# Two semaphores in place of one for the later rows of the fine index: what the change does to an adjacency kernel on one core

## The reference, cut to what matters

```python
def _L0_gnn_ref(x, adj, mask, W1, b1, W2, b2):
    ...
    nd = adj_d > 0
    vals = jnp.where(nd[..., None], x[:, None, :, :], jnp.inf)
    s = jnp.sort(vals, axis=2)
    nv = nd.sum(2)
    agg = jnp.zeros_like(x)
    for tau, w in zip(TAUS, WTS):
        pos = jnp.asarray(tau, x.dtype) * jnp.maximum(nv - 1, 0).astype(x.dtype)
        lo = jnp.floor(pos).astype(jnp.int32)
        hi = jnp.ceil(pos).astype(jnp.int32)
        ...
        agg = agg + jnp.asarray(w, x.dtype) * (v_lo + frac * (v_hi - v_lo))
    ...
    h = jax.nn.relu(out @ W1 + b1)
    y = h @ W2 + b2
...
x = _layernorm(x + _L0_gnn_ref(x, adj, nodemask, ...), axis=-1)
```

## Time and profile before

| | us |
|---|---|
| median of 3 runs | 3416.59 |
| lowest and highest of them | 3411.93, 3427.28 |
| the profiled execution, its own time | 3415.25 |
| span of that execution in the trace | 3413.5 |
| busy: PE, DVE, ACT | 2304.1, 2806.8, 1993.9 |

### The profile page before, as it was taken

How to read it: one execution, slowest core, us unless ns; L and a number is a source line. 1 busy time by engine, 2 the same in 40 slices (tenths; PEclk the granted TensorE clock), 3 DMA queues, 4 the chain that set the end, 5 groups by cost and what they waited for, 6 DMA issues and landing times.

```text
span 3413.5 us, 45704 instructions
## 1 busy us (share of the span) xinstructions
PE 2304.1 (67%) x16234; PEld 1004.3 (29%) x16234; DVE 2806.8 (82%) x5398; ACT 1993.9 (58%) x3077; POOL 12.4 (0%) x24
## 2 busy tenths in 40 slices
PE   0000015667878787878878787878778787866996
PEld 0000002223333333323333333323233333213764
DVE  7999998978788888879788887878797888635776
ACT  2112432466867676867768676867677676741232
POOL 0000000000000000000000000000000000000000
PEclk6555557788888888989889888888888888876777
DMA  3001000000000101010000101010000000000011
GB/s 63 0 0 48 6 0 19 7 23 19 20 19 20 31 11 28 13 32 11 28 19 19 20 20 30 11 33 9 31 12 27 19 20 19 5 23 25 26 37 37
DMA packets 126915, 72.05 MB, mean 21 GB/s; under 512 B 95512, under 2 KB 110058, under 8 KB 126698
## 3 DMA queue, kind: packets, MB, share of 16 engines
q1 hardware_dynamic: 122570, 68.23, 7.8%
q10 hardware_dynamic: 4128, 1.05, 0.2%
HBM read 41.05 MB, written 15.58 MB: 17 GB/s over the span
## 4 chain that ended last, share of the span: by engine, by line
PE 38%; SPq 20%; DVE 20%; ACT 12%; issue 7%; DMA 2%; DVEq 0%; ACTq 0%
SPq L403 20%; PE ring L623 8%; PE rows L662 7%; ACT hot L1075 6%; PE found_bank L674 5%; PE bcast L636 4%; DVE keys L1324 2%; DVE keys L1323 2%; ACT prod L1068 2%; PE bank L916 2%; DVE delta L1364 1%; DVE delta L1362 1%; DVE perm L1366 1%; DVE perm L1367 1%; PE bcast L754 1%
## 5 line engine op out<-in xcount | busy, mean ns | idle before, releaser
L1075 ACT ACTIVATE hot<-bcast,consts 128x1024 f16<-128x1024 f32 x744 | 831.5, 1118 | 129.3 <-PE bcast L636 129.1
L623 PE MATMUL ring<-member,neigh_t 128*128 128x512 bf16 x2048 | 543.8, 410 | 22.5 <-DVE member L1412 13.0
L1068 ACT ACTIVATE prod<-rows 128x512 f32<-128x512 f32 x720 | 431.6, 599 | 195.0 <-PE rows L662 195.0
L662 PE MATMUL rows<-hot,table 128*64 128x512 f16 x3072 | 526.2, 424 | 0.0
L651 PE MATMUL rows<-fine_rows,consts 32*128 32x512 bf16 x768 | 318.6, 415 | 207.7 <-DMA fine_rows<-turned 207.4
L636 PE MATMUL bcast<-idx_t,consts 32*128 32x512 f16 x1488 | 310.8, 414 | 158.5 <-ACT hot L1075 157.1
L623 PEld LDWEIGHTS ring<-member,neigh_t 128*128 128x128 bf16 x2048 | 193.3, 104 | 342.0 <-issue 135.5
L561 PE MATMUL ring<-identb,adj_b 128*128 128x128 bf16 x256 | 35.1, 274 | 368.9 <-ACT adj_b L971 357.6
L674 PE MATMUL found_bank<-prod,consts 128*32 128x512 f32 x1536 | 239.8, 701 | 11.2 <-ACT prod L1068 10.5
L1493 DVE TENSOR_SCALAR picked<-cnt,above 128x960 bf16<-128x960 f16 x192 | 78.7, 467 | 193.8 <-PE bcast L745 180.4
L1521 DVE TENSOR_TENSOR picked<-picked 128x3072 uint16<-128x3072 uint16 (+2 forms) x192 | 209.5, 1091 | 11.2
(11 more groups left out here) (347 smaller groups left out, 4424.1 us busy)
## 6 DMA issues: line engine op xcount, KB each, us to landing
late<-in_adj_dram SPq DMA_DIRECT2D x16, 1024.0 KB, 5.4
adjt_d<-neigh_t SPq DMA_DIRECT2D x16, 512.0 KB, 2.7
fine_rows<-turned SPq DMA_DIRECT2D x512, 8.0 KB
fine_rows<-turned SPq DMA_DIRECT2D x512, 16.0 KB
turned<-adjt_d SPq DMA_DIRECT2D x16, 512.0 KB, 3.7
adj_s<-adjt_d SPq DMA_DIRECT2D x16, 512.0 KB, 3.6
xt_d<-keys SPq DMA_DIRECT2D x2, 1024.0 KB, 10.5
parts_d<-parts SPq DMA_DIRECT2D x4, 512.0 KB, 6.9
```

The costliest lines, as they stand in the source:

```text
L623: ins = mm(ring[u % 2][:, :], kept_t[:, j, P * i:P * i + P], member[:, j, n // 2, 512 * (n % 2):512 * (n % 2) + 512], start=(j == 0), stop ...
L662: ins = mm(rows[u % 2][C * h:C * h + C, :], table[:, s, GROUPS * h + g8, :], hot[:, u % HOT, h, :], start=False, stop=(s == 1), skip_group ...
L1068: run(prod[:, u % DEEP, :], rows[u % 2][:, :], ACT.Relu).then_inc(S["prod_by_act"], 1)
L1075: run(hot[:, u % HOT].rearrange(flat), spread_bank(l, u)[0][:, 0:2, :].rearrange(flat), ACT.Relu, bias=eq_bias[:, :]).then_inc(S["hot_read ...
```

## The change

A new semaphore `odd_in` takes the 16 transfers that carry k = 1, the odd half of the first quantile's pair; `later_in` keeps the 32 that carry k = 2 to 5. TensorE waits for `odd_in` at unit 8 and for `later_in` at unit 16, which is the first that reads k = 2. SP waits for both before it goes on. No transfer, matmul or other instruction changes its place. The line numbers of `place_fine` and of what stands behind `away` move by one to three.

```diff
                 for g8 in range(GROUPS):
                     for n in range(2):
-                        fine_part(g8, n, 1, 0, 1).then_inc(S["later_in"], 16)
+                        fine_part(g8, n, 1, 0, 1).then_inc(S["odd_in"], 16)
                 hold(sp, S["idxT_ev"], TURNS * l + 4, S["sp_passed"])
                 for s in range(2):
                     for g8 in range(GROUPS):
                         for n in range(2):
                             fine_part(g8, n, s, 1, 3).then_inc(S["later_in"], 16)
-                hold(sp, S["later_in"], 768 * l + 768, S["sp_passed"])
+                hold(sp, S["odd_in"], 256 * l + 256, S["sp_passed"])
+                hold(sp, S["later_in"], 512 * l + 512, S["sp_passed"])
...
                 if u == GROUPS:
-                    pe.wait_ge(S["later_in"], 768 * l + 768)
+                    pe.wait_ge(S["odd_in"], 256 * l + 256)
+                if u == 2 * GROUPS:
+                    pe.wait_ge(S["later_in"], 512 * l + 512)
```

More of the change, by code:

```diff
@@ L332, in build @@
             tile_read cnt_read mask_used idx_ready idxT_ps idxT_ev table_in adjl_in bc_ps place_ps
-            later_in hot_ready row_ps prod_by_act prod_by_dve found_ps nb_read sum_ev xt_out span_ready unspan_clear unspan_in x_t_in x1T_ps x1T_ev gcn_ev h_ps h_ev y_ps z_ready
+            odd_in later_in hot_ready row_ps prod_by_act prod_by_dve found_ps nb_read sum_ev xt_out span_ready unspan_clear unspan_in x_t_in x1T_ps x1T_ev gcn_ev h_ps h_ev y_ps z_ready
             sd_ready x1_ready tr_ps split_ready g_ps dve_chain out_done sp_passed pe_passed w23_ready wT_ps
```

## The result

The changed kernel takes 3193.98 us (median of 4 runs, 3187.44 to 3202.8) against 3416.11 before: a ratio of 0.9347, interval 0.9315 to 0.9379. 3195 was forecast. Its profiled execution took 3195.59 us, with a span of 3193.8.

A forecast was written before the change was run, and what follows sets the result against it. The prediction took SP's serial issuing to bound the kernel, making TensorE and then VectorE wait each pass. It took 177.4 + 34 + 9 = 220.4 us off 3415.25, saying 3195; forecast 3183 to 3208 (65 in 100), range 3176 to 3232.

The forecast's parts named there:

- The stall: TensorE's wait at unit 8 for `fine_rows` transfers goes in whole in 15 graphs: 177.4 us, 11.8 each.
- The clock behind the stall: Unit 8 to unit 9 regains the higher TensorE clock: 2.25 us a pass, 34 us for 15 graphs.
- TensorE's 14.1 as the smaller of the two: A pass shortens by TensorE's 14.1 us, since VectorE can give 15.3 from its waits at tile 3 and L1421.
- VectorE's 9.5 us to spare: VectorE, busy 132 us, still fits in a pass shortened to about 141.5 us, with 9.5 to spare.
- The last graph: Units 8 to 15 run before the last landing, gaining 11.2 us; 2.2 are given back at unit 16: 9.0.
- The sum: 177.4 + 34 + 9 = 220.4 us off 3415.25 gives 3194.9; the median stands 1.3 higher; 3195 was said.
- VectorE alone: VectorE becomes the bound at once, only its 12.0 us a pass appear: 3226; 17 in 100 with the clock's case.
- Half a stall: The wait stays in part at unit 8 or 16, half of the 177.4 us is left: 3315; 5 in 100.
- Less clock and slower: Denser TensorE work gets a lower clock; at 0.75 a pass is 6.8 us longer: 3517; 3 in 100.

The follow-up runs named there:

- experiment 2: Changed kernel with the wait for the last 32 transfers at unit 10 instead of unit 16: 3331.35 us, ratio 0.9742.
- experiment 10: Changed kernel with the wait for the last 32 transfers at unit 12 instead of unit 16: 3184.64 us, ratio 0.9308.
- experiment 1: Kernel before the change, with 48 matmuls on TensorE ahead of unit 8's wait, so it works during the stall: 3398.44 us, ratio 0.9941.
- experiment 6: Changed kernel with nine short memsets added on VectorE ahead of tile 3: 3256.46 us, ratio 0.9529.
- experiment 5: Changed kernel with 12 more matmuls on TensorE ahead of unit 12 in every graph: 3218.71 us, ratio 0.9417.
- experiment 3: Changed kernel with the split waits in the last graph alone; elsewhere unit 8 waits for both semaphores: 3413.28 us, ratio 0.9984.
- experiment 9: The changed kernel run again, unchanged: 3203.71 us, ratio 0.9374.
- experiment 4: Changed kernel with GpSimd instead of SP issuing the last 32 transfers in the last graph: 3194.01 us, ratio 0.9332.
- experiment 7: Changed kernel with SP and GpSimd sharing the 64 transfers of the last graph: 3168.91 us, ratio 0.9278.
- experiment 8: Changed kernel with two more matmuls ahead of each of units 13 to 30 in the first 15 graphs: 3227.13 us, ratio 0.9446.
- experiment 11: Kernel with the last graph's transfers shared by SP and GpSimd, plus one matmul ahead of each of units 15 to 22: 3169.8 us, ratio 0.9268.

## Why the prediction was right, step by step

**The stall (177.4 us): right.** All of it went in 15 graphs. Its arithmetic held: the 32nd transfer's landing at 23.3 us behind the first (2780.40 against 2757.12, in the last graph, where it is waited for; forecast 23.5), unit 8 asking at 34.4 (forecast 1612.5 - 1577.3 = 35.2), unit 16 with 9.5 us to spare (forecast 10). Experiments 2 and 10 moved the place of the wait, and in the loop the stall came back at unit 10 and not at unit 12, as this count says.

**The clock behind the stall (34 us): the sum came out, the term is less certain than it looked.** What the loop gained beyond the stall is 211.8 - 177.4 = 34.4 us (its two ends: 2757.12 - 650.92 against 2969.18 - 651.16). But alone, in experiment 1, the higher clock behind the stall gave 20 us, 13 to 27; in experiment 2 each pass lost 3.0 us beyond the stall, 45 over 15. The 2.3 us between the first two units behind the stall are the clock's in both. What I did not count is that the clock later in the pass also moves: in experiment 1 it was 0.68 and not 0.80 beside tile 3, and in the changed kernel two of 13 passes are some 5 us longer than the rest. Over a whole pass the clock was 0.87 before (l = 6); it is 0.93 in the changed kernel's pass of l = 6 and 0.87 in that of l = 4. So 34.4 is the sum of passes that gained more and passes that gained less, and its closeness to 34 is partly luck. It is also no pure clock term, since VectorE's own pace bounds what a pass can gain (experiment 6). The rule in the Trainium skill (TensorE: Matmul & The Clock Gate, section "HAM oscillation — how this bites in real kernels"), that a DMA wait in a loop is paid again at each pass by the lower clock, agrees with experiment 2, where a wait of 5.6 us made the pass 8.6 us longer. In experiment 1, where the wait was filled, the clock held for the next units, and about 20 of the 34 us were gained.

**TensorE's 14.1 as the smaller of the two: the size right, the reason half right.** The pass shortened by 14.1 us (211.8 / 15), and L1424's wait fell from 3.2 to 1.1 us a pass as forecast (to about 1). But a mean hides two kinds. In most passes L1424 waits for 1 us or nothing; in the long ones TensorE and ScalarE are late by 4.2. Experiments 5 and 6 show both engines within about 1 us of the bound. VectorE's 9.5 us to spare, as I put it, were not spare: 3.4 us more of its work lengthened a pass by 4.2. Busy time against the length of a pass was the wrong comparison. In the pass of l = 6 VectorE is busy 131.1 of 139.95 us, and the waits that the profile names add up to 2.8; the other 6 us lie in short gaps between its instructions, which the profile puts down to no other engine.

**The last graph (9.0 us): right in kind, the size not settled.** 7.6 us in the changed kernel, 8.3 in experiment 3, 4.3 in experiment 9: 0.7 to 4.7 below the forecast. The waits were forecast at 7 and 12 us and are 6.13 and 11.99; the restart at unit 16 cost 4.95 - 2.76 = 2.19 (forecast 2.2).

**The sum.** 177.4 + 34 + 9 give 3194.9 against the profiled execution; with the 1.3 us up to the median, which the forecast speaks of, that is 3196.2 and not 3195. The difference is too small to matter.

**The rivals.** VectorE alone (3226) needs L1424's wait to stay or another to appear; it fell. Half a stall (3315): experiment 2 shows what it looks like, at 3331. Less clock and slower: busy time of TensorE fell by 52.9 us, so the clock went up in sum. But a part of this rival exists: two passes with the stall gone have a lower clock than the others and take 146 us, at a price of 5 to 6 us each and not of the whole gain.

**What stays open.** Why one pass drops its clock early and the next does not, with the same instructions, was not settled. The number of such passes in a profiled execution was 2, 3, 5, 2 and 0 for kernels whose loop issues the same instructions (the changed kernel, experiments 9, 4, 7 and 10). They are not scattered at random. From 60 to 90 us behind the first transfer the granted clock is 0.66 in all 12 long passes, and 0.76 to 0.86 in the 53 others from l = 1 to 13. And each of the 12 follows directly on a pass of 140.65 to 140.77 us. So the length of a pass goes with where the clock falls in it, and something passes on from one pass to the next. That the fall of the clock is the cause, and not itself a result of some other delay, is argued from the slower matmuls and not shown by an edit: experiments 8 and 11 were meant to show it and did not.

## What to carry to other kernels

Give each group of transfers that has its own first reader its own semaphore, and wait where it is read; then count, from the first issue, when each group lands and when its reader asks. Where the issuing itself is waited for, as in the last graph, spread the issues over an idle engine's queue: that took another 20 to 23 us off the last graph here. And before spending idle time or busy-share "room", add a few instructions to each engine in turn, at the place where you would spend it: here that showed in two runs what shares of busy time had not. Where an edit is worth less than 10 us of 3200, one trace of each kernel is not enough.

## What the runs showed of the hardware

- **Equal passes of unequal length.** The same instructions took 139.0 to 146.2 us a pass, and the granted clock of one stretch went with it (0.83 or 0.60 on average). The medians of one kernel, measured on two chips, stood 10 us apart (3193.98 and 3203.71), which is more than some of the edits here are worth.
- **Filling a stall keeps the clock, and it falls later.** With 48 matmuls in the stall (47 in the trace) the clock was 1.00 for the next 30 us and then 0.68 where it had been 0.80, in the pass shown.
- **The issuing sets the pace, not the moving.** A transfer of 8 or 16 KB takes SP 0.71 us and GpSimd 0.53 to 0.56 us of its queue, and both issued at once without slowing each other (32 each in 23.12 and 17.11 us). The last of SP's 64 landed 2.03 us behind its issue. The DMA share was 0.08 to 0.15 in the windows of the kernels before and after, and 0.19 where both queues issued.
